# Two steps of lead between the engines of an edge network, in place of one

## The chip, the cores and the metric

The kernel runs on one core of a Trainium2 chip. The metric is the device time of one execution in microseconds, and a kernel's time is the median of its runs.

## The reference

Four graph networks run one after the other on a graph of 12,500 nodes with 128 features and 212,500 edges (sorted by destination, self-loops among them). The change touches only the second of them. It computes, for h the normalized node features:

```python
edge_input = jnp.concatenate([x[row], x[col], edge_attr], axis=-1)
h = jax.nn.silu(edge_input @ eW1 + eb1)
m_ij = jax.nn.silu(h @ eW2 + eb2)
agg = jax.ops.segment_sum(m_ij, row, num_segments=x.shape[0])
```

Here row is the source node of an edge, col its destination, and edge_attr has 16 numbers an edge. Then agg goes through a node network. Everything is float32.

## The kernel before, in words

The kernel works the whole computation in one program of many blocks. A block gives each engine its own list of instructions, and semaphores order them. Ahead of the edge network, the program has sorted the edges by source into buckets of 112 nodes and cut them into 1776 tiles of 128 edges (KT). It wrote a record for each edge to the table `rec_d` in HBM: 16 attributes, the destination's number, and the place of the source within its bucket. It also multiplied the node features with the two halves of eW1 once a node, into the tables `tab` (destination's part) and `tab_b` (source's part). So the first layer of an edge is a sum of one gathered row of `tab`, one row picked out of a 112-row window of `tab_b`, and the attributes' product.

The block of the edge network, printed below, goes over 444 quads of four tiles. Quad n uses slot s = n % 8 of a ring of eight (LR). Its steps are:

- SP, line 1840, brings the records of the quad (one DMA of 512 rows of 72 bytes) and, line 1843, four windows of `tab_b`. It waits until PE's first layer (`pe_z`) has finished quad n - 8, which had the slot. This is called a bring.
- POOL, line 1860, issues four indirect DMAs, one a tile, that gather the destination rows of `tab`. It waits for the records, since they hold the row numbers.
- DVE, line 1910, makes a one-hot of each edge's source within the bucket, from the record, next to the attributes: `comb`, 128 columns a tile.
- PE, line 1936, transposes `comb` into PSUM; ACT, line 1963, copies it to `combT`, one of two buffers.
- PE, lines 1927 and 1928, the first layer z: a transpose of the gathered rows, to which `a_win` times `combT` is added in PSUM. ACT, line 1968, applies silu into `h1`.
- PE, line 1943, the second layer; DVE, line 1891, adds the bias into `msg`; ACT, line 1972, silu in place.
- PE, line 1951, multiplies the messages with the one-hot (112 columns), which sums them by source node; DVE, line 1901, adds each of the four results into the 112 columns of F that begin at the tile's first node. That number is loaded from the table `bases` into registers by `at_base`.

No planner orders the work. The order is written out by hand in `step(n, s, h)` of DVE, PE and ACT: within one step, the parts for different quads follow each other, and a test `inside(n, d)` drops those that fall off the ends. Before the change PE's step n does: first layer of quad n, transposes of n + 1, second layer of n - 1, message sums of n - 2. DVE's step n does: bias of n - 1, adds of n - 2, one-hots of n + 2. ACT's step n does: copy of n + 1, silu of n, silu of n - 1. Each buffer between two engines (`combT`, `h1`, `msg` and the PSUM banks) is double. `steps` runs 55 turns of a hardware loop of eight steps, with 4 steps written out ahead of it and 4 behind.

Of the kernel before, what the change touches and what calls it, by code (L numbers as in the profile page):

```python
# [29 lines left out]
P = 128  # L30
# [24 lines left out]
BW = 112  # L55
NB = NP // BW
RW = 18
RQ = 4
KT = 1776
LR = 8  # L60
NT_B = (KT + P - 1) // P
NQ = KT // RQ
# [19 lines left out]
def build(nc, t, out, stop=99):  # L82
    ctx = ExitStack()
    with ctx:
# [48 lines left out]
        ident = sb("ident", [P, P])  # L133
        iota_row = sb("iota_row", [P, P])
# [23 lines left out]
        def fslot(n):  # L158
# [432 lines left out]
        W = [wts[:, n * P:(n + 1) * P] for n in range(5)]  # L591
# [3 lines left out]
        def tile_of(buf, j, w=P):  # L595
            return buf[:, j * w:(j + 1) * w]
# [1204 lines left out]
        if stop <= 6: return  # L1801

        CW = P + 2
        at[0] = 0
        comb = [in_hs(RQ * CW) for _ in range(LR)]
        a_win = [hs[:, at[0] + s * RQ * P:at[0] + (s + 1) * RQ * P] for s in range(LR)]
# [2 lines left out]
        combT = [wk[:, (LR + d) * RQ * P:(LR + d + 1) * RQ * P] for d in range(2)]  # L1809
        h1, msg = ([in_hs(RQ * P) for _ in range(2)] for _ in range(2))  # L1810
# [3 lines left out]
        with nc.Block() as block:  # L1814
# [15 lines left out]
        at_base = lambda n, eng: nc.values_load_multi_w_load_instructions(  # L1830
            bases[0:1, bass.ds(n * RQ, RQ)], engines=[eng], min_val=0, max_val=NP,
            skip_runtime_bounds_check_because="the table holds first nodes of buckets")[1]
        with nc.Block() as block:
# [35 lines left out]

            def steps(eng, step):  # L1870

                for n in range(-2, 2):
                    step(n, n % LR, n // LR)
                with eng.Fori(0, (NQ - 4) // LR) as i:
                    for u in range(LR):
                        step(i * LR + u + 2, (u + 2) % LR, i + (u + 2) // LR)
                for n in range(NQ - 2, NQ + 2):
                    step(n, n % LR, n // LR)

            inside = lambda n, d: not isinstance(n, int) or 0 <= n + d < NQ  # L1880
            round_of = lambda n, h, s, d: h + (s + d) // LR

            @block.vector
            def _(v):
                def step(n, s, h):

                    if inside(n, -1):
                        d = (s - 1) % 2
                        v.wait_ge(pe_m.sem, pe_m.after(n))
                        v.wait_ge(pe_s.sem, pe_s.after(n - 2))  # L1890
                        v.tensor_tensor(msg[d].rearrange("p (u f) -> p u f", f=P), bank(4 + d).rearrange("p (u f) -> p u f", f=P),  # L1891
                                        every(bias_b[1], RQ), ALU.add).then_inc(z2_ready.sem, 1)
                    if inside(n, -2):
                        d = s % 2
                        first = at_base(n - 2, mybir.EngineType.DVE)
                        v.wait_ge(pe_s.sem, pe_s.after(n - 1))
                        for u in range(RQ):
                            cols = F[:, bass.ds(first[u], BW)]

                            v.wait_ge(added.sem, added.after((n - 2) * RQ + u))  # L1900
                            v.tensor_tensor(cols, cols, PS[:, (6 + d) * 512 + u * BW:(6 + d) * 512 + (u + 1) * BW], ALU.add)\  # L1901
                                .then_inc(added.sem, 1)
                    if inside(n, 2):
                        s2 = (s + 2) % LR
                        v.wait_ge(rec_in[s2].sem, rec_in[s2].after((round_of(n, h, s, 2) + 1) * 16))

                        v.wait_ge(pe_s.sem, pe_s.after(n + 3 - LR))
                        for u in range(RQ):
                            c = u * CW
                            last = v.tensor_scalar(comb[s2][:, c:c + BW], iota_row[:, 0:BW], comb[s2][:, c + P + 1:c + P + 2], None,  # L1910
                                                   ALU.is_equal)
                        last.then_inc(onehot_ready.sem, 1)
                steps(v, step)

            @block.tensor
            def _(pe):
                def step(n, s, h):
                    d = s % 2
                    if inside(n, 0):

                        pe.wait_ge(turned_in.sem, turned_in.after(n + 1))
                        pe.wait_ge(win_in[s].sem, win_in[s].after((h + 1) * (16 * RQ)))
                        pe.wait_ge(got[s].sem, got[s].after((h + 1) * (16 * RQ)))
# [6 lines left out]
                    if inside(n, 1):  # L1930
                        s1 = (s + 1) % LR
                        pe.wait_ge(onehot_ready.sem, onehot_ready.after(n + 2))
                        pe.wait_ge(rec_in[s1].sem, rec_in[s1].after((round_of(n, h, s, 1) + 1) * 16))
                        pe.wait_ge(turned_in.sem, turned_in.after(n))
                        for u in range(RQ):
                            last = pe.transpose(tile_of(bank(2 + s1 % 2), u), comb[s1][:, u * CW:u * CW + P], ident[:, :])  # L1936
                        last.then_inc(pe_t.sem, 1)
                    if inside(n, -1):
                        d1 = (s - 1) % 2
                        pe.wait_ge(h1_ready.sem, h1_ready.after(n))  # L1940
                        pe.wait_ge(z2_ready.sem, z2_ready.after(n - 2))
                        for u in range(RQ):
                            last = pe.matmul(tile_of(bank(4 + d1), u), tile_of(h1[d1], u), W[2], start=True, stop=True)
                        last.then_inc(pe_m.sem, 1)
                    if inside(n, -2):
                        s2 = (s - 2) % LR
                        pe.wait_ge(msg_ready.sem, msg_ready.after(n - 1))
                        pe.wait_ge(added.sem, added.after((n - 3) * RQ))
                        for u in range(RQ):
                            c = (6 + d) * 512 + u * BW  # L1950
                            last = pe.matmul(PS[:, c:c + BW], tile_of(msg[d], u), comb[s2][:, u * CW:u * CW + BW],
                                             start=True, stop=True)
                        last.then_inc(pe_s.sem, 1)
                steps(pe, step)

            @block.scalar
            def _(act):
                def step(n, s, h):
                    if inside(n, 1):
                        d1 = (s + 1) % 2  # L1960
                        act.wait_ge(pe_t.sem, pe_t.after(n + 2))
                        act.wait_ge(pe_z.sem, pe_z.after(n))
                        act.copy(combT[d1], bank(2 + d1)).then_inc(turned_in.sem, 1)
                    if inside(n, 0):
                        d = s % 2
# [3 lines left out]
                    if inside(n, -1):  # L1969
                        d = (s - 1) % 2  # L1970
                        act.wait_ge(z2_ready.sem, z2_ready.after(n))
# [446 lines left out]
```

## Time and profile before

| | |
|---|---|
| median of 3 runs | 19,315.99 us (19,311.27 to 19,325.33) |
| profiled execution: its time | 19,314.88 us |
| profiled execution: span | 19,313.1 us |
| busy in the span: PE / PE weight loads / DVE / ACT / POOL | 7930.3 / 6299.9 / 6589.2 / 1534.9 / 11,514.0 us |
| the edge network's block | about 8446 to 11,862 us of the span |

Engines: PE is TensorE (its weight loads, PEld, overlap its matmuls), DVE VectorE, ACT ScalarE, POOL GpSimd, SP the engine that only issues DMAs here. A line such as L1936 is a line of the kernel. "idle before" is the time in which the engine did nothing ahead of these instructions, and behind "<-" stands what ended it: an instruction or a DMA, "issue" where the profile shows nothing, "remote" where a semaphore rose at that moment but the profile can't tell by whom. A queue's name ends in q (SPq). Matmuls in float32 show as more instructions than the code has. The clock is the share of full speed that TensorE was granted; 1.00 is 2.4 GHz, 0.50 is 1.2 GHz.

### The profile page before, as it was taken

To read this page: it belongs to the slowest core of one execution; us is meant where nothing else is said; L and a number is where in the kernel's file an instruction comes from. 1 tells how busy PE (TensorE), PEld (TensorE's weight loads), DVE (VectorE), ACT (ScalarE), POOL (GpSimd) and SP (SyncE) were. 2 spreads that over 40 slices of the span, in tenths; PEclk is the share of its full clock that TensorE was granted. 3 is DMA by queue.
4 is the path that set the end of the run, shared out by engine and by line. 5 is a ranking of instruction groups with operands and counts; after the bars stand their busy time and mean duration, and the time that the engine had idled before them with its cause. 6 is when DMAs were issued, how large, how long until landed. Compare 5 with 4: busy or idle time off the path is not lost. (4 is left out here: it accounts for less than half of the span.)

```text
span 19313.1 us, 144155 instructions
## 1 busy us (share of the span) xinstructions
PE 7930.3 (41%) x37282; PEld 6299.9 (33%) x37282; DVE 6589.2 (34%) x14435; ACT 1534.9 (8%) x3978; POOL 11514.0 (60%) x12117
## 2 busy tenths in 40 slices
PE   2222222222223333335565555444454444345444
PEld 1222222222222111125555554333333333233333
DVE  4444443444444333323333334222232222322222
ACT  3000000000000100012222222000000000100000
POOL 4666664666664666664454444666656666466666
PEclk5555555555555555568888887555555555555555
DMA  5222223111111111122222223111111111111112
GB/s 139 54 52 52 52 52 53 45 44 44 44 45 31 18 26 28 23 44 70 68 71 70 68 69 71 47 47 47 60 52 47 47 46 47 39 53 47 46 47 56
DMA packets 1301502, 993.98 MB, mean 51 GB/s; under 512 B 751003, under 2 KB 1121912, under 8 KB 1298942
## 3 DMA queue, kind: packets, MB, share of 16 engines
q0 software_dynamic: 387456, 692.11, 14.4%
q1 hardware_dynamic: 691046, 272.90, 6.0%
q10 hardware_dynamic: 222520, 23.31, 0.9%
q8 instruction: 211, 3.46, 0.1%
q14 instruction: 269, 2.20, 0.0%
HBM read 868.44 MB, written 132.38 MB: 52 GB/s over the span
## 5 line engine op out<-in xcount | busy, mean ns | idle before, releaser
L819 POOL DMA_INDIRECT wk<-tab,srcT x4992 | 4709.8, 943 | 2535.3 <-issue 1460.1
L920 POOL DMA_INDIRECT hs<-tab_g,srcT x3328 | 3148.0, 946 | 1886.0 <-issue 951.2
L843 PE MATMUL PS<-wk 128*128 128x128 f32 x9984 | 2579.5, 439 | 3757.3 <-DMA wk<-tab,srcT 3666.1
L843 PEld LDWEIGHTS PS<-wk 128*128 128x128 f32 x9984 | 2208.5, 325 | 4389.6 <-DMA wk<-tab,srcT 4281.8
L872 DVE TENSOR_TENSOR F<-F,PS 128x512 f32 x1248 | 857.3, 687 | 5475.2 <-PE PS L843 3723.9
L1860 POOL DMA_INDIRECT wk<-tab,hs x1776 | 1677.3, 944 | 1722.4 <-DMA hs<-rec_d 1128.2
L1780 POOL DMA_INDIRECT rec_d<-hs x1664 | 1621.1, 974 | 827.2 <-issue 522.1
L1111 DVE TENSOR_TENSOR F<-F,PS 128x126 f32 x3328 | 950.4, 286 | 2571.2 <-issue 1188.1
L1067 PE MATMUL PS<-wk,hs 128*128 128x128 f32 x6656 | 1276.4, 370 | 740.4 <-DVE hs L1096 562.3
L1067 PEld LDWEIGHTS PS<-wk,hs 128*128 128x128 f32 x6656 | 1186.4, 276 | 832.3 <-issue 777.4
L1047 PE MATMUL PS<-ident,wk 128*128 128x128 f32 (+1 forms) x104 | 45.2, 435 | 2245.9 <-ACT wk L991 2141.5
L1936 PE MATMUL PS<-ident,hs 128*128 128x128 f32 x1776 | 360.6, 337 | 1440.4 <-DVE hs L1910 1230.0
L1767 PE MATMUL PS<-hs 128*128 128x448 bf16 x416 | 225.1, 541 | 1585.5 <-DVE hs L1651 1010.0
L1891 DVE TENSOR_TENSOR hs<-PS,wts 128x512 f32<-128x512 f32 x444 | 307.0, 691 | 1477.9 <-remote 661.8
L834 PE MATMUL PS<-wk 1*128 1x512 bf16 x1248 | 745.8, 598 | 131.0 <-DVE wk L784 130.2
L784 DVE TENSOR_TENSOR wk<-PS,locT 128x1024 f32<-128x1024 f32 x624 | 758.9, 1217 | 0.1
L1047 PEld LDWEIGHTS PS<-ident,wk 128*128 128x128 f32 (+1 forms) x104 | 14.8, 142 | 2274.1 <-ACT wk L991 2169.3
L1901 DVE TENSOR_TENSOR F<-F,PS 128x112 f32 x1776 | 481.4, 271 | 798.6 <-remote 429.0
L1936 PEld LDWEIGHTS PS<-ident,hs 128*128 128x128 f32 x1776 | 232.5, 167 | 1522.6 <-DVE hs L1910 985.5
L1651 DVE TENSOR_TENSOR hs<-PS,hs 128x448 f32<-128x448 f32 x416 | 256.4, 616 | 1200.1 <-remote 1007.3
L1928 PE MATMUL PS<-wk,hs 128*128 128x128 f32 x3552 | 653.2, 286 | 0.0
L1767 PEld LDWEIGHTS PS<-hs 128*128 128x128 bf16 x416 | 43.0, 103 | 1829.7 <-DVE hs L1651 1140.1
(398 smaller groups left out, 11156.9 us busy)
## 6 DMA issues: line engine op xcount, KB each, us to landing
hs<-tab_b SPq DMA_DIRECT2D x1776, 56.0 KB
wk<-tab,srcT POOLq DMA_INDIRECT x4992
hs<-tab_g,srcT POOLq DMA_INDIRECT x3328
wk<-tab,hs POOLq DMA_INDIRECT x1776
rec_d<-hs POOLq DMA_INDIRECT x1664
rec_d<-F SPq DMA_DIRECT2D x1, 15984.0 KB
hs<-rec_d SPq DMA_DIRECT2D x444, 36.0 KB
hs<-attr_d ACTq DMA_DIRECT2D x208, 64.0 KB
```

The lines of the kernel that those rows point to most:

```text
L784: return v.tensor_tensor(dst, iota_ps[:, 0:w].unsqueeze(1).broadcast_to([P, HALF, w]), loc.unsqueeze(2).broadcast_to([P, HALF, w]), ALU.is ...
L819: pool.indirect_dma_start(gbuf[g % 4 * QUAD + u], None, table, bass.IndirectOffsetOnAxis(srcT[:, edges_of(k)], 0))\
L834: pe.matmul(bank(g % NBK), zeros[:, 0:P], zeros, start=True, stop=False, skip_group_check=True)
L843: last = pe.matmul(to, rows[u], onehot[j], start=False, stop=u == QUAD - 1, skip_group_check=True)
L872: v.tensor_tensor(cols, cols, bank(g % NBK), ALU.add).then_inc(added.sem, 1)
L920: pool.indirect_dma_start(gt[n % 2][:, j, :], None, table, bass.IndirectOffsetOnAxis(srcT[:, n * BT + j:n * BT + j + 1], 0)).then_inc(half ...
L1067: last = pe.matmul(tile_of(in_bank(g), u), gt[s][:, j, 0:D], onehot[j % (2 * HALF)], start=True, stop=True)
L1111: v.tensor_tensor(cols, cols, in_bank(k // QUAD)[:, c + 1:c + P - 1], ALU.add).then_inc(added.sem, 1)
L1780: pool.indirect_dma_start(rec_d, bass.IndirectOffsetOnAxis(slot_i[r][:, j:j + 1], 0), tile_of(rec[r], j, RW), None).then_inc(scattered[r]. ...
L1860: pool.indirect_dma_start(tile_of(b_rows[s], u), None, tab, bass.IndirectOffsetOnAxis(comb[s].bitcast(I32)[:, c:c + 1], 0))\
L1928: last = pe.matmul(z, tile_of(a_win[s], u), tile_of(combT[d], u), start=False, stop=True)
L1936: last = pe.transpose(tile_of(bank(2 + s1 % 2), u), comb[s1][:, u * CW:u * CW + P], ident[:, :])
```

## The change

The leads and lags are set by two constants, MID = 2 and FAR = 4. PE's step n does: first layer of n, transposes of n + 2, second layer of n - 2, message sums of n - 4. DVE's step n does: bias of n - 2, adds of n - 4, one-hots of n + 4. ACT's: copy of n + 2, silu of n, silu of n - 2. The buffers stay double, their index is now that of the step, and the numbers that the semaphores are compared with follow the lags. The loop takes 54 turns of eight steps, with 8 steps written out ahead and 12 behind. The programs of SP and POOL are as they were. Cut to its core:

```diff
+        MID, FAR = 2, 4
-                for n in range(-2, 2):
+                turns = (NQ - 2 * FAR) // LR
+                for n in range(-FAR, FAR):
                     step(n, n % LR, n // LR)
-                with eng.Fori(0, (NQ - 4) // LR) as i:
+                with eng.Fori(0, turns) as i:
...
-                for n in range(NQ - 2, NQ + 2):
+                for n in range(FAR + turns * LR, NQ + FAR):
...
-                    if inside(n, -1):
-                        d = (s - 1) % 2
-                        v.wait_ge(pe_m.sem, pe_m.after(n))
-                        v.wait_ge(pe_s.sem, pe_s.after(n - 2))
+                    if inside(n, -MID):
+                        d = s % 2
+                        v.wait_ge(pe_m.sem, pe_m.after(n - MID + 1))
+                        v.wait_ge(pe_s.sem, pe_s.after(n - MID - 1))
...
-                    if inside(n, -2):
+                    if inside(n, -FAR):
...
-                        v.wait_ge(pe_s.sem, pe_s.after(n - 1))
+                        v.wait_ge(pe_s.sem, pe_s.after(n - FAR + 1))
...
-                        v.wait_ge(pe_s.sem, pe_s.after(n + 3 - LR))
+                        v.wait_ge(pe_s.sem, pe_s.after(n + FAR + 1 - LR))
...
-                        pe.wait_ge(onehot_ready.sem, onehot_ready.after(n + 2))
+                        pe.wait_ge(onehot_ready.sem, onehot_ready.after(n + MID + 1))
...
-                        pe.wait_ge(turned_in.sem, turned_in.after(n))
+                        pe.wait_ge(turned_in.sem, turned_in.after(n + MID - 1))
...
-                        pe.wait_ge(h1_ready.sem, h1_ready.after(n))
-                        pe.wait_ge(z2_ready.sem, z2_ready.after(n - 2))
+                        pe.wait_ge(h1_ready.sem, h1_ready.after(n - MID + 1))
+                        pe.wait_ge(z2_ready.sem, z2_ready.after(n - MID - 1))
...
-                        pe.wait_ge(msg_ready.sem, msg_ready.after(n - 1))
-                        pe.wait_ge(added.sem, added.after((n - 3) * RQ))
+                        pe.wait_ge(msg_ready.sem, msg_ready.after(n - FAR + 1))
+                        pe.wait_ge(added.sem, added.after((n - FAR - 1) * RQ))
```

## Rows read from the trace of the kernel before

**Rows 1.** Groups by line in the edge network's stretch (8440 to 11870): busy us, mean ns | idle before.
```profile
L1860 POOL DMA_INDIRECT wk<-tab,hs x1776 | 1677.3, 944 | 1722.4 <-DMA hs<-rec_d 1128.2 <-issue 523.5 <-PE PS L1928 70.7
...
L1927 PE MATMUL PS<-ident,wk 128*128 128x128 f32 x1776 | 512.1, 288 | 36.3 <-issue 21.0 <-ACT wk L1963 15.2
...
L1936 PE MATMUL PS<-ident,hs 128*128 128x128 f32 x1776 | 360.6, 337 | 1440.4 <-DVE hs L1910 1230.0 <-issue 210.4
```

**Rows 2.** Waits of SP's queue there: total us, times, longest us.
```profile
SPq L1840 <- remote: 775.3, 155, 9.5
SPq L1840 <- PE PS L1928: 718.6, 199, 6.1
```

**Rows 3.** Timeline of SP: start us, length us, issues; the 1st, 16th and 444th bring.
```profile
8444.47 0.00 SPq L1840 DMA_DIRECT2D hs<-rec_d  x1
...
8540.19 0.39 SPq L1840 DMA_DIRECT2D hs<-rec_d  x1
...
11808.12 0.40 SPq L1840 DMA_DIRECT2D hs<-rec_d  x1
```

**Rows 4.** Stretches: length, busy us (instructions) of PE, PEld, DVE, ACT, POOL, clock, DMA, GB/s.
```profile
8544.00:11808.00 3264.00, 1925.74 (x13665) 1842.67 (x13664) 1088.39 (x3840) 728.38 (x1280) 1612.17 (x1707) 0.83 0.30 69
11824.00:11855.00 31.00, 23.57 (x204) 22.46 (x202) 16.01 (x57) 10.52 (x19) 0.00 (x0) 1.00 0.00 1
...
8800.00:9200.00 400.00, 233.92 (x1690) 223.32 (x1689) 134.53 (x477) 90.07 (x159) 198.97 (x212) 0.84 0.29 70
10000.00:10400.00 400.00, 239.36 (x1686) 228.84 (x1685) 134.93 (x474) 89.99 (x159) 200.31 (x212) 0.83 0.29 70
```

**Rows 5.** Timeline of PE and DVE, one of the last quads: start, length, [idle before].
```profile
11831.00 0.66 PE L1936 MATMUL PS<-ident,hs 128*128 128x128 f32 x4 [1.29 <-DVE hs L1910]
...
11833.66 1.48 DVE L1901 TENSOR_TENSOR F<-F,PS 128x112 f32 x4 [0.37 <-PE PS L1951]
...
11835.08 0.84 DVE L1910 TENSOR_SCALAR hs<-iota_row,hs 128x112 f32<-128x112 f32 x4
...
11836.17 0.63 PE L1936 MATMUL PS<-ident,hs 128*128 128x128 f32 x4 [1.41 <-DVE hs L1910]
```

**Rows 6.** Timeline of all engines from 9008 to 9025, a long quad.
```profile
9008.53 1.87 SPq L1843 DMA_DIRECT2D hs<-tab_b  x4
...
9010.81 0.94 POOL L1860 DMA_INDIRECT wk<-tab,hs  x1 [4.82 <-DMA hs<-rec_d]
...
9013.60 4.60 SPq L1843 DMA_DIRECT2D hs<-tab_b  x4
...
9013.81 0.66 PE L1936 MATMUL PS<-ident,hs 128*128 128x128 f32 x4 [1.18 <-DVE hs L1910]
...
9014.30 1.06 PE L1943 MATMUL PS<-wts,hs 128*128 128x128 f32 x8
...
9019.72 0.94 POOL L1860 DMA_INDIRECT wk<-tab,hs  x1 [0.30 <-issue]
9020.82 0.69 DVE L1891 TENSOR_TENSOR hs<-PS,wts 128x512 f32<-128x512 f32 x1 [7.07 <-remote]
...
9024.90 1.11 PE L1936 MATMUL PS<-ident,hs 128*128 128x128 f32 x4 [7.33 <-DVE hs L1910]
```

**Rows 7.** Timeline in the earlier stage that scatters the records.
```profile
7023.05 0.97 POOL L1780 DMA_INDIRECT rec_d<-hs  x1 [0.30 <-issue]
7023.07 0.62 DVE L1651 TENSOR_TENSOR hs<-PS,hs 128x448 f32<-128x448 f32 x1 [19.91 <-remote]
```

**Rows 8.** Timelines of PE and POOL in the opening of the edge network.
```profile
8455.32 0.63 PE L1928 MATMUL PS<-wk,hs 128*128 128x128 f32 x2
...
8466.56 0.95 POOL L1860 DMA_INDIRECT wk<-tab,hs  x1 [5.17 <-PE PS L1928]
...
8505.63 0.98 POOL L1860 DMA_INDIRECT wk<-tab,hs  x1 [5.27 <-PE PS L1928]
...
8543.65 0.39 PE L1928 MATMUL PS<-wk,hs 128*128 128x128 f32 x2
```

More of the change, by code:

```diff
@@ L1870, in steps @@
             def steps(eng, step):
-                for n in range(-2, 2):
+                turns = (NQ - 2 * FAR) // LR
+                for n in range(-FAR, FAR):
                     step(n, n % LR, n // LR)
-                with eng.Fori(0, (NQ - 4) // LR) as i:
+                with eng.Fori(0, turns) as i:
                     for u in range(LR):
-                        step(i * LR + u + 2, (u + 2) % LR, i + (u + 2) // LR)
-                for n in range(NQ - 2, NQ + 2):
+                        step(i * LR + u + FAR, (u + FAR) % LR, i + (u + FAR) // LR)
+                for n in range(FAR + turns * LR, NQ + FAR):
                     step(n, n % LR, n // LR)
@@ L1892, in step @@
                                         every(bias_b[1], RQ), ALU.add).then_inc(z2_ready.sem, 1)
-                    if inside(n, -2):
+                    if inside(n, -FAR):
                         d = s % 2
-                        first = at_base(n - 2, mybir.EngineType.DVE)
-                        v.wait_ge(pe_s.sem, pe_s.after(n - 1))
+                        first = at_base(n - FAR, mybir.EngineType.DVE)
+                        v.wait_ge(pe_s.sem, pe_s.after(n - FAR + 1))
                         for u in range(RQ):
@@ L1898, in step @@
                             cols = F[:, bass.ds(first[u], BW)]
-                            v.wait_ge(added.sem, added.after((n - 2) * RQ + u))
+                            v.wait_ge(added.sem, added.after((n - FAR) * RQ + u))
                             v.tensor_tensor(cols, cols, PS[:, (6 + d) * 512 + u * BW:(6 + d) * 512 + (u + 1) * BW], ALU.add)\
                                 .then_inc(added.sem, 1)
-                    if inside(n, 2):
-                        s2 = (s + 2) % LR
-                        v.wait_ge(rec_in[s2].sem, rec_in[s2].after((round_of(n, h, s, 2) + 1) * 16))
-                        v.wait_ge(pe_s.sem, pe_s.after(n + 3 - LR))
+                    if inside(n, FAR):
+                        s4 = (s + FAR) % LR
+                        v.wait_ge(rec_in[s4].sem, rec_in[s4].after((round_of(n, h, s, FAR) + 1) * 16))
+                        v.wait_ge(pe_s.sem, pe_s.after(n + FAR + 1 - LR))
@@ L1908, in step @@
                         for u in range(RQ):
                             c = u * CW
-                            last = v.tensor_scalar(comb[s2][:, c:c + BW], iota_row[:, 0:BW], comb[s2][:, c + P + 1:c + P + 2], None,
+                            last = v.tensor_scalar(comb[s4][:, c:c + BW], iota_row[:, 0:BW], comb[s4][:, c + P + 1:c + P + 2], None,
                                                    ALU.is_equal)
@@ L1929, in step @@
                         last.then_inc(pe_z.sem, 1)
-                    if inside(n, 1):
-                        s1 = (s + 1) % LR
-                        pe.wait_ge(onehot_ready.sem, onehot_ready.after(n + 2))
-                        pe.wait_ge(rec_in[s1].sem, rec_in[s1].after((round_of(n, h, s, 1) + 1) * 16))
-                        pe.wait_ge(turned_in.sem, turned_in.after(n))
+                    if inside(n, MID):
+                        s2 = (s + MID) % LR
+                        pe.wait_ge(onehot_ready.sem, onehot_ready.after(n + MID + 1))
+                        pe.wait_ge(rec_in[s2].sem, rec_in[s2].after((round_of(n, h, s, MID) + 1) * 16))
+                        pe.wait_ge(turned_in.sem, turned_in.after(n + MID - 1))
@@ L1935, in step @@
                         for u in range(RQ):
-                            last = pe.transpose(tile_of(bank(2 + s1 % 2), u), comb[s1][:, u * CW:u * CW + P], ident[:, :])
+                            last = pe.transpose(tile_of(bank(2 + d), u), comb[s2][:, u * CW:u * CW + P], ident[:, :])
                         last.then_inc(pe_t.sem, 1)
-                    if inside(n, -1):
-                        d1 = (s - 1) % 2
-                        pe.wait_ge(h1_ready.sem, h1_ready.after(n))
-                        pe.wait_ge(z2_ready.sem, z2_ready.after(n - 2))
+                    if inside(n, -MID):
+                        pe.wait_ge(h1_ready.sem, h1_ready.after(n - MID + 1))
+                        pe.wait_ge(z2_ready.sem, z2_ready.after(n - MID - 1))
@@ L1942, in step @@
                         for u in range(RQ):
-                            last = pe.matmul(tile_of(bank(4 + d1), u), tile_of(h1[d1], u), W[2], start=True, stop=True)
+                            last = pe.matmul(tile_of(bank(4 + d), u), tile_of(h1[d], u), W[2], start=True, stop=True)
                         last.then_inc(pe_m.sem, 1)
-                    if inside(n, -2):
-                        s2 = (s - 2) % LR
-                        pe.wait_ge(msg_ready.sem, msg_ready.after(n - 1))
-                        pe.wait_ge(added.sem, added.after((n - 3) * RQ))
+                    if inside(n, -FAR):
+                        s4 = (s - FAR) % LR
+                        pe.wait_ge(msg_ready.sem, msg_ready.after(n - FAR + 1))
+                        pe.wait_ge(added.sem, added.after((n - FAR - 1) * RQ))
@@ L1949, in step @@
                         for u in range(RQ):
                             c = (6 + d) * 512 + u * BW
-                            last = pe.matmul(PS[:, c:c + BW], tile_of(msg[d], u), comb[s2][:, u * CW:u * CW + BW],
+                            last = pe.matmul(PS[:, c:c + BW], tile_of(msg[d], u), comb[s4][:, u * CW:u * CW + BW],
                                              start=True, stop=True)
@@ L1958, in step @@
                 def step(n, s, h):
[L1959 to L1963, printed above, removed]
+                    d = s % 2
+                    if inside(n, MID):
+                        act.wait_ge(pe_t.sem, pe_t.after(n + MID + 1))
+                        act.wait_ge(pe_z.sem, pe_z.after(n + MID - 1))
+                        act.copy(combT[d], bank(2 + d)).then_inc(turned_in.sem, 1)
                     if inside(n, 0):
-                        d = s % 2
                         act.wait_ge(pe_z.sem, pe_z.after(n + 1))
@@ L1968, in step @@
                         act.activation(h1[d], bank(d), ACT.Silu).then_inc(h1_ready.sem, 1)
-                    if inside(n, -1):
-                        d = (s - 1) % 2
-                        act.wait_ge(z2_ready.sem, z2_ready.after(n))
+                    if inside(n, -MID):
+                        act.wait_ge(z2_ready.sem, z2_ready.after(n - MID + 1))
                         act.activation(msg[d], msg[d], ACT.Silu).then_inc(msg_ready.sem, 1)
```

## The prediction

> **What bounds the kernel now.** I looked first at the groups by line in the stretch of the edge network, since the diff touches nothing else. It lasts from about 8446 to 11862 us, 3416 us of the span, for 444 quads. PE waits for nothing but one thing there: the transposes of line 1936, ahead of which it idles 1440.4 us, 1230.0 us of that until DVE's one-hots of line 1910. Ahead of the first layer's products (line 1927), where the gathered rows are waited for, it idles 36.3 us [rows 1]. So gathers are in time, and POOL is not late: it idles 1722.4 us, mostly until the records of the slot that it is to fill have landed. Those are brought by SP, and SP waits 718.6 us for PE's first layer to free the slot and 775.3 us for the same semaphore with the releaser shown as "remote" [rows 2]. The ring of eight slots is thus full, and PE's chain sets the pace.
>
> The table of stretches gives that pace. Between the 16th bring (8540.19) and the last (11808.12) lie 428 quads in 3267.9 us, 7.635 us a quad [rows 3]. In 3264 us PE is busy 1925.74 us, that is 4.5 us a quad at a mean clock of 0.83; DVE 1088.39 (2.5), ACT 728.38 (1.7), POOL 1612.17 [rows 4]. No engine is full.
>
> The timeline then shows two kinds of quad. At the very end, where nothing is brought or gathered, one quad follows another in 5.17 us (11831.00 to 11836.17), and the chain is plain: the sums' matmuls end, DVE adds four tiles (11833.66, 1.48 us), makes four one-hots (11835.08, 0.84 us), PE transposes at 11836.17 after 1.41 us idle [rows 5]. PE itself works 23.57 us in 31 us there, 204 matmuls at 32 a quad, so 3.7 us a quad at full clock [rows 4].
>
> In the middle every second or third quad is far longer, as the one whose transposes come at 9013.81 and the next at 9024.90, 11.1 us later. PE starts the second layer at 9014.30 and takes 1.06 us, and DVE, which waits for just that, starts at 9020.82, after 7.07 us of idle "<-remote": PE's signal came 5.5 us late. PE's next transposes, which need DVE's one-hots, wait 7.33 us and run at the low clock (1.11 us, against 0.66 before). In the same microseconds SP's four issues of line 1843 take 4.60 us in place of 1.87, and POOL gathers without a break, eight in a row (9010.81 to 9019.72); its stop and the late signal come together [rows 6]. A clean bring of SP (9008.53) fell into a break of POOL. I read this as **a freeze**: where SP brings while POOL gathers back to back, signals of PE arrive late and SP crawls. It isn't a matter of PE's load: in the earlier stage that scatters the records, where PE has little to do, DVE waits 19.91 us "<-remote" (to 7023.07) in a run of POOL that still goes on at 7023.05, with 0.30 us between scatters [rows 7].
>
> **The change part by part.**
> 1. Slack. Today PE's step n needs the one-hots, first layer and messages of step n-1 of DVE and ACT; after the change those of step n-2. The 1.41 us ahead of the transposes in a clean quad goes, and the step falls to what is busiest: PE 3.7 us [rows 4], DVE 0.69 + 1.48 + 0.84 = 3.0 us plus its gaps [rows 5, 6], POOL 4 x (0.944 + 0.30) = 4.98 us [rows 1, 6]. By this POOL's 4.98 us is the floor.
> 2. In a freeze PE can go on two steps in place of one before it starves, and DVE has up to two steps of released work.
> 3. What is late next: SP's brings. Nothing of SP or POOL is moved, no DMA and no queue; but the opening shows what the two do when PE doesn't hold them. There SP has free slots, and 15 brings take from 8444.47 to 8540.19, 6.38 us a quad [rows 3]; POOL gathers 12 times, stops some 5 us (5.17 at 8466.56, 5.27 at 8505.63), and so on [rows 8]. That is the pace of bring and gather against one another, and I take it for the pace after: 6.38 us. It is bounded below by POOL's 4.98 and above, short of a loss (rival C), by today's 7.635. I take 6.38 because it is measured in this very loop with both at work, and because PE can just follow: two runs and stops of POOL lie between 8466.56 and 8505.63, 19.5 us for each 12 gathers [rows 8], in which three quads need 3 x 3.7 us of PE and about 3 x 3.5 of DVE (an estimate, the 3.0 with gaps), and of the 19.5 us a freeze leaves the 5 us stop, the 3 us until the next sets in, and two steps carried over.
> 4. Costs. The one-hots of quad n+4 reuse a slot whose last reader is the message sum of quad n-4, which DVE's adds just ahead wait for anyway: no new wait. The semaphore waits, register loads and instructions of a step stay as many; 20 steps stand outside the loop in place of 8, which I cost at nothing, since each step is the same instructions (0 to 3 us). At the end four quads' sums are left in place of two; the last of DVE's bias and four adds cost 0.69 + 1.48 us a quad [rows 5, 6], some 3 us more after what PE's saved gaps hide; 0 to 10. At the start four one-hots are made ahead, under the same first records, POOL's first gathers and SP's first brings: nothing.
>
> The sum, for the profiled execution's 19314.88 us (span 19313.1, and within 1.2 us of the median): 428 x (7.635 - 6.38) = 537 us off, 3 us on: **18,781 us**. The opening and the last eight quads I leave as they are.
>
> A rule that can be set against this: the Trainium skill, page "DMA: Bandwidth & Descriptors", section "SWDGE vs HWDGE vs iDMA", has it that transfers issued by SP don't touch the descriptor rings that GpSimd writes, and are immune to what disturbs those. By that rule alone nothing should slow SP's brings, and the floor would be POOL's. The trace disagrees on the outcome, with 4.60 against 1.87 us for the same four issues; no row shows which part of the chip they meet in.
>
> **The rivals.**
> A. *The pace is held from outside, and stays.* For it: the pace is steady over long stretches: 400 us from 8800 and 400 us from 10000 hold 1690 and 1686 matmuls [rows 4]; it is as if freezes came after so many transfers and gave out a fixed rate. Then a smoother pipeline only brings the next freeze sooner. Against: in the opening brings went through at 6.38 us, and 7.6 us also comes out of POOL's 5.0 a quad and one stop of 5 us for every two quads. Time: 19,318, with a spread of 60 us either way, since 0.1 us a quad is already 43 us.
> B. *No collision counts once PE has slack; POOL is the bound.* 428 x (7.635 - 4.98) = 1136 us off, 3 on: 18,182. For it: the stops of POOL are then rare, and the ring of eight can cover a freeze. Against: the opening had free slots too, and POOL stopped every 12 gathers.
> C. *Slower: longer runs of POOL make longer freezes.* The place is the run-and-stop cycle. In the opening, the first layer's products of quad 0 begin their last pair at 8455.32 and those of quad 8 at 8543.65 [rows 8], 11.0 us a quad, 1.8 quads to a cycle of 19.5 us: PE was slower under POOL's continuous run than it is now. Slack gives POOL these runs back. The point that decides is 19.5 / 7.635 = 2.55 quads a cycle: if PE gets fewer than that with slack two, the time goes up. At 2.4 it is 8.13 us a quad, 428 x 0.49 = 210 us on: 19,528 with the 3 of the end. Against: a full ring stops POOL, and that brings back the present pattern.
>
> **How the numbers follow.** My forecast's case (5.4 to 7.3 us a quad, 18,360 to 19,170) gets 0.55, A 0.25, B 0.07, C 0.13. The range: 18,300 to 19,350 takes in the first, nearly all of A, and leaves out B, much of C and the first case's tail, some 0.2. A measurement of this kernel can tell 0.2% (39 us) from nothing. Faster by more: 0.55 + 0.07 + 0.07 of A = 0.69. Within: 0.15 of A and 0.01 of C, 0.16. Slower: 0.03 of A and 0.12 of C, 0.15.
>
> **What would show it.** Right: the stretch shrinks from 3416 to about 2880 us; the idle time before line 1936 falls from 1440 to under 500 us, and part of it turns up before line 1927 as a wait for the gathers; POOL's runs grow to 12 gathers and its idle falls under 1300 us; brings come every 6.4 us; SP's waits for line 1928 shrink. A shows as the same 7.6 us with the idle time moved to another line of PE. B shows as POOL without stops. C shows as runs of 12 and more with under 2.5 quads to each. The forecast is wrong if "remote" waits fill the two steps of slack each time, or if the loop's pace in the opening was set by something that only the opening has.

## The result and the profile after

| | before | after |
|---|---|---|
| median | 19,320.66 us (4 runs) | 19,000.15 us (4 runs, 18,990.61 to 19,016.99) |
| profiled execution: its time | 19,314.88 us | 18,990.61 us |
| profiled execution: span | 19,313.1 us | 18,988.8 us |
| ratio after / before | | 0.9838, interval 0.9827 to 0.9850 |

The change wins 320 us. The direction was forecast, and the time lies in the range, which was 1050 us wide; the gain is 320 of the 534 us forecast.

The lines of the code have moved by one to five: POOL's gathers are L1861, SP's brings L1841 and L1844, DVE's bias, adds and one-hots L1893, L1903 and L1912, PE's first layer L1929 and L1930, transposes L1938, second layer L1944, sums L1952, ACT's copy L1964. First the groups by line in the edge network (8440 to 11600), to be held against [rows 1]:

```profile
L1861 POOL DMA_INDIRECT wk<-tab,hs x1776 | 1685.6, 949 | 1410.6 <-DMA hs<-rec_d 731.0 <-issue 533.6 <-PE PS L1930 133.3
L1930 PE MATMUL PS<-wk,hs 128*128 128x128 f32 x3552 | 807.7, 317 | 296.0 <-issue 294.1
...
L1944 PE MATMUL PS<-wts,hs 128*128 128x128 f32 x3552 | 645.0, 327 | 157.2 <-issue 155.5
L1952 PE MATMUL PS<-hs 128*128 128x112 f32 x3552 | 598.3, 312 | 121.5 <-issue 118.9 <-DVE F L1903 1.7
...
L1929 PE MATMUL PS<-ident,wk 128*128 128x128 f32 x1776 | 551.0, 310 | 141.0 <-issue 134.6 <-ACT hs L1968 4.4 <-DMA wk<-tab,hs 1.0
...
L1938 PE MATMUL PS<-ident,hs 128*128 128x128 f32 x1776 | 360.5, 325 | 204.7 <-issue 124.2 <-DVE hs L1912 80.1
L1893 DVE TENSOR_TENSOR hs<-PS,wts 128x512 f32<-128x512 f32 x444 | 306.5, 690 | 1762.0 <-remote 1530.5 <-PE PS L1952 128.3 <-issue 97.1
```

The idle time ahead of the transposes is down from 1440.4 to 204.7 us. PE waits for hardly anything any more (80.1 us for the one-hots, of which 72 are the wait for the first quad's). DVE's late signals have not gone: its bias waits 1530.5 us for "remote", against 661.8 before. They only no longer hold PE. And yet it idles 920 us in all (296.0 + 157.2 + 121.5 + 141.0 + 204.7), nearly all of it "issue": the profile shows nothing that it waited for, in the midst of its lists of matmuls.

SP's waits there answer to [rows 2]. Ahead of a bring SP waits for one semaphore only, that of PE's first layer, so both lines are waits for a slot of the ring: 26.2 us are put down to PE, 921.2 to "remote". What has changed is that the slot is mostly free by then and the signal late. Of the 416 brings from the 25th to the 440th, 317 start over 2 us after the end of the first layer that frees their slot (half of them over 4.9 us after it); before it was 150, and half started within 0.8 us.

```profile
SPq L1841 <- remote: 921.2, 216, 12.1
...
SPq L1841 <- PE PS L1930: 26.2, 20, 2.0
```

Then SP's timeline at the 16th and the 444th bring [rows 3], and the same loop as a stretch [rows 4]:

```profile
8535.92 0.39 SPq L1841 DMA_DIRECT2D hs<-rec_d  x1
...
11496.34 0.40 SPq L1841 DMA_DIRECT2D hs<-rec_d  x1
```

```profile
8547.00:11481.00 2934.00, 2139.16 (x13495) 1971.00 (x13495) 1065.74 (x3799) 719.53 (x1268) 1607.30 (x1694) 0.80 0.34 76
```

2960.4 us for 428 quads are **6.92 us a quad**, against 7.635. The bookkeeping closes: the brings gain 3267.9 - 2960.4 = 307.5 us. From the last bring to the last add there are 40.5 us (to 11536.8) in place of 54.2 (to 11862.3), 14 more. And the first bring comes at 8439.93 in place of 8444.47, 4.5 us that the change has no part in. That is 326, and the two profiled executions differ by 324. Where did the rest of the removed wait go? 1236 us went from the idle time ahead of the transposes (1440.4 to 204.7). Of these, 679 came back as idle time ahead of PE's other lines (296.0 + 157.2 + 121.5 + 141.0 = 715.7, against the 36.3 of line 1927 before, [rows 1]), and 213 as slower instructions (PE is busy 2139.16 us in the stretch, 1925.74 before [rows 4]; the transposes of the gathered rows take 310 ns in place of 288). That leaves 344, near the 321 that the brings and the end gain.

Last, the timeline of all engines around one freeze, which answers to [rows 6]:

```profile
9500.98 1.06 PE L1944 MATMUL PS<-wts,hs 128*128 128x128 f32 x8
...
9503.77 0.23 PEld L1929 LDWEIGHTS PS<-ident,wk 128*128 128x128 f32 x1
9504.22 0.95 POOL L1861 DMA_INDIRECT wk<-tab,hs  x1 [0.30 <-issue]
9505.17 0.27 PE L1929 MATMUL PS<-ident,wk 128*128 128x128 f32 x1 [1.04 <-issue]
9505.18 0.19 PEld L1930 LDWEIGHTS PS<-wk,hs 128*128 128x128 f32 x1 [1.19 <-issue]
...
9505.90 0.19 PEld L1930 LDWEIGHTS PS<-wk,hs 128*128 128x128 f32 x1 [0.53 <-issue]
...
9506.61 0.37 PE L1930 MATMUL PS<-wk,hs 128*128 128x128 f32 x1 [1.05 <-issue]
...
9507.32 0.18 PEld L1938 LDWEIGHTS PS<-ident,hs 128*128 128x128 f32 x1 [1.24 <-issue]
9508.02 1.01 PE L1938 MATMUL PS<-ident,hs 128*128 128x128 f32 x4 [1.04 <-issue]
...
9508.16 0.59 ACT L1964 COPY wk<-PS 128x512 f32<-128x512 f32 x1 [7.79 <-remote]
9508.27 0.69 DVE L1893 TENSOR_TENSOR hs<-PS,wts 128x512 f32<-128x512 f32 x1 [6.30 <-remote]
...
9508.83 1.91 PE L1944 MATMUL PS<-wts,hs 128*128 128x128 f32 x8
...
9509.45 0.95 POOL L1861 DMA_INDIRECT wk<-tab,hs  x1 [3.04 <-DMA hs<-rec_d]
```

Here is what the added slack ran into. While POOL gathers, ACT and DVE get no signal (7.79 and 6.30 us "<-remote"), as before: the second layer that DVE's bias waits for ended at 9502.04 (9500.98 + 1.06), and the bias starts at 9508.27. PE now has work left that waits for neither, and begins it. But its own instructions, matmuls and weight loads alike, then start only in steps of 0.70 us or twice that: 9503.77, 9505.17, 9505.90, 9506.61, 9507.32, 9508.02. POOL's run ends at 9506.41 (9509.45 less its 3.04 idle), and 1.6 us later all three go on together. The matmuls behind it run at the half clock: eight in 1.91 us, where eight take 1.06 at full clock [rows 6], and the granted clock of that stretch is 0.50:

```profile
9508.00:9510.00 2.00, 1.98 (x10) 1.97 (x10) 1.45 (x4) 1.84 (x4) 0.55 (x1) 0.50 0.23 67
```

This is no single case. Counted over the whole loop, 899 of PE's idle gaps, 643 us, stand ahead of matmuls that wait for no semaphore. In the kernel before there is not one. In its long quads PE stood at its wait for the one-hots when the slow stretch would have come (idle from 9017.57 to 9024.90 [rows 6]), so this could not be seen in its trace.

The rows of before hold one more fact that bears on the forecast's idea of a freeze. In the earlier stage of [rows 7], PE's transposes of line 1737 end at 6999.20 (6998.78 + 0.42), and ACT's copy of them starts at 7019.57, 20 us later, in a run of POOL's scatters:

```profile
6998.78 0.42 PE L1737 MATMUL PS<-ident,F 128*128 128x128 f32 x1
...
7019.57 0.91 ACT L1616 COPY wk<-PS 128x896 f32<-128x896 f32 x1 [24.23 <-remote]
```

From 7000 to 7025 us SP issues nothing at all. The issues of that stretch are these:

```profile
rec_d<-hs POOLq DMA_INDIRECT x19
hs<-attr_d ACTq DMA_DIRECT2D x2, 64.0 KB
```

So a signal of PE comes late there without any bring of SP.

### The profile page after: what moved, and what is told of

The parts are those of the page before. It is cut to its first block and busy times, and to the rows that moved or that the text cites. A ratio compares the mean times of both kernels' runs of the same rounds, so it can differ in the third digit from the quotient of the medians.

```text
span 18988.8 us, 142973 instructions
## 1 busy us (share of the span) xinstructions
PE 8166.6 (43%) x37282; PEld 6450.6 (34%) x37282; DVE 6582.3 (35%) x14435; ACT 1534.0 (8%) x3978; POOL 11546.0 (61%) x12117
## 5 line engine op out<-in xcount | busy, mean ns | idle before, releaser
L819 POOL DMA_INDIRECT wk<-tab,srcT x4992 | 4720.8, 946 | 2526.4 <-issue 1460.2
L1861 POOL DMA_INDIRECT wk<-tab,hs x1776 | 1685.6, 949 | 1410.6 <-DMA hs<-rec_d 731.0
L1067 PE MATMUL PS<-wk,hs 128*128 128x128 f32 x6656 | 1275.5, 370 | 737.4 <-DVE hs L1096 578.1
L1067 PEld LDWEIGHTS PS<-wk,hs 128*128 128x128 f32 x6656 | 1185.6, 276 | 829.5 <-issue 769.0
L1930 PE MATMUL PS<-wk,hs 128*128 128x128 f32 x3552 | 807.7, 317 | 296.0 <-issue 294.1
L1893 DVE TENSOR_TENSOR hs<-PS,wts 128x512 f32<-128x512 f32 x444 | 306.5, 690 | 1762.0 <-remote 1530.5
L1930 PEld LDWEIGHTS PS<-wk,hs 128*128 128x128 f32 x3552 | 664.4, 227 | 347.7 <-issue 346.4
L1944 PE MATMUL PS<-wts,hs 128*128 128x128 f32 x3552 | 645.0, 327 | 157.2 <-issue 155.5
L1952 PE MATMUL PS<-hs 128*128 128x112 f32 x3552 | 598.3, 312 | 121.5 <-issue 118.9
```

The costliest lines, as they stand in the source:

```text
L819: pool.indirect_dma_start(gbuf[g % 4 * QUAD + u], None, table, bass.IndirectOffsetOnAxis(srcT[:, edges_of(k)], 0))\
L1067: last = pe.matmul(tile_of(in_bank(g), u), gt[s][:, j, 0:D], onehot[j % (2 * HALF)], start=True, stop=True)
L1861: pool.indirect_dma_start(tile_of(b_rows[s], u), None, tab, bass.IndirectOffsetOnAxis(comb[s].bitcast(I32)[:, c:c + 1], 0))\
L1944: last = pe.matmul(tile_of(bank(4 + d), u), tile_of(h1[d], u), W[2], start=True, stop=True)
```

## The experiments

They were run in four groups, each on one chip with the kernel before beside it, and every ratio is against the kernel before of its own group. That took 19,332.8 us in the first group (runs e1 to e4), 19,323.3 in the second (e5 to e8), 19,328.5 in the last (e12), and **16,057.4 us** in the third (e9 to e11), which fell on another chip. The second group and e12 had the same chip, the first a different one with the same kernel time. "Pace" is us a quad over the 414 quads between the ends of the first layer of the 17th and of the 431st; it is 7.63 for before and 6.93 for after, counted so.

**e1: only the two leads ahead of the first layer.** The constants are split in four; one-hots four ahead and transposes two ahead, as after; second layer one and sums two behind, as before.

```diff
-        MID, FAR = 2, 4
+        OH, TR, L2, SC = 4, 2, 1, 2
```

> One-hots four quads ahead and turning two ahead as in the changed kernel, but the second layer one quad and the message sums two quads behind, as before. If slack counts as the smallest lag on any of PE's waits, the lag of one step that stays on the second layer and the sums keeps PE tied to the last step of ACT and DVE: under a quarter of the 320 us gained, 19,240 us or more. Rival: the trace of before shows PE waiting only for the one-hots, so this half alone brings the gain: about 19,000 us.

Measured: 19,032.53 us, ratio 0.9840 (0.9823 to 0.9856), pace 6.96. The second layer and the sums of PE, groups by line of this run:

```profile
L1945 PE MATMUL PS<-wts,hs 128*128 128x128 f32 x3552 | 646.5, 327 | 186.9 <-issue 162.4 <-ACT hs L1971 21.9 <-DVE hs L1893 0.8
L1954 PE MATMUL PS<-hs 128*128 128x112 f32 x3552 | 604.6, 315 | 156.9 <-issue 125.3 <-ACT hs L1975 21.5 <-DVE F L1903 8.7
```

Half of the change gives all of its gain that can be told from noise (0.9840 against 0.9838 and, in e12, 0.9847). The smallest lag of the four doesn't count: with a lag of one PE waits for `h1` and `msg` 43 us in all.

**e2: only the two lags behind.**

```diff
-        MID, FAR = 2, 4
+        OH, TR, L2, SC = 2, 1, 2, 4
```

> The other half alone: second layer two and message sums four quads behind, one-hots two and turning one ahead as before. By the theory of the smallest lag: PE still waits for the one-hots of the step before, no gain, 19,280 to 19,330 us. Rival, that late signals on the way back (second layer to bias to sums) are what costs: about 19,100 us.

Measured: 19,335.67 us, ratio 0.9997 (0.9988 to 1.0007), pace 7.59. The wait of before is all there, ahead of the transposes:

```profile
L1938 PE MATMUL PS<-ident,hs 128*128 128x128 f32 x1776 | 351.9, 331 | 1426.3 <-DVE hs L1912 1142.3 <-issue 284.1
```

DVE's one-hots stand last in its step, behind the bias that waits for PE's late signal. Only where they are made further ahead does PE not wait for them; what DVE and ACT owe PE behind the first layer came in time at both lags tried (e1). So the other half of the change does nothing by itself.

**e7: the one-hots alone, one quad further ahead.**

```diff
-        MID, FAR = 2, 4
+        OH, TR, L2, SC = 3, 1, 1, 2
```

> The kernel before with one thing changed: one-hots three quads ahead in place of two; turning one ahead, second layer one and sums two behind as before. The one-hots that PE waits for come then from DVE's step before the last. If that wait alone was the cost: 19,000 to 19,070 us. If the copy of the turned one-hots, which still comes from the step before and needs a signal of PE, takes its place: 19,200 to 19,320 us, with the idle time moved to the first layer's line.

Measured: 19,140.73 us, ratio 0.9903 (0.9887 to 0.9920), pace 7.24: some 183 of 300 us. The wait has moved to the next thing that is only one step ahead, ACT's copy of the transposed one-hots:

```profile
L1929 PE MATMUL PS<-ident,wk 128*128 128x128 f32 x1776 | 623.6, 351 | 988.3 <-ACT wk L1967 960.4 <-issue 28.0
```

So one more quad of lead for the one-hots brings part of the gain, and the rest comes with the lead of the transposes and the fourth quad of the one-hots (e1, pace 6.96). These two were not taken apart.

**e3: after, without POOL's gathers.** POOL's block and PE's wait for it are left out, so the first layer adds whatever is in the rows' buffers.

```diff
-            @block.gpsimd
-            def _(pool):
-                def gather(n, s, i):
...
-                        pe.wait_ge(got[s].sem, got[s].after((h + 1) * (16 * RQ)))
```

> The changed kernel with the gathers of POOL left out in the edge network (the first layer reads what stands in the buffers; the output is not the reference's). If POOL's back-to-back gathers cause the freezes, waits shown as remote nearly vanish, SP's issues take 1.87 us each four, and the pace is PE's 3.7 to 4.3 us a quad: stage 1650 to 1950 us, total 17,550 to 17,850 us. If the pace is held by something else (a rate of records or transfers, of which gathers are a small part), quads still take over 6 us: 18,600 us or more.

Measured: 17,498.41 us, ratio 0.9048 (0.9030 to 0.9066), pace 3.54. A stretch of it, same columns as [rows 4]:

```profile
8600.00:9000.00 400.00, 400.00 (x3619) 400.00 (x3618) 286.22 (x1017) 205.00 (x339) 0.00 (x0) 1.00 0.35 77
```

In this stretch PE is never idle, at full clock; in the whole block no wait of PE's matmuls, of DVE or of ACT is shown as "remote" or "issue". SP's four issues take 1.87 us all but three times (all in the first eleven quads). The freezes of this block come with POOL's gathers. Whether it is POOL's issuing or the transfers that it starts, the run can't tell, as both are gone.

**e6: before, without POOL's gathers** (the same part left out).

> The kernel before, with POOL's gathers left out (output not the reference's). Without freezes its chain shows alone: the 5.0 to 5.2 us a quad of the last quads of its trace, so the stage takes 2230 to 2320 us and the kernel 18,130 to 18,230 us, against 17,498 for the changed kernel without gathers. If instead the chain costs nothing without freezes, both are equal: 17,500 us.

Measured: 18,143.66 us, ratio 0.9387 (0.9368 to 0.9405), pace 5.00. PE's transposes:

```profile
L1916 PE MATMUL PS<-ident,hs 128*128 128x128 f32 x1776 | 290.8, 286 | 619.8 <-DVE hs L1891 548.7 <-DMA hs<-rec_d 71.1
```

Where nothing freezes and no gather bounds, the slack is worth 18,144 - 17,498 = 645 us (two chips, whose kernel before differs by 10 us), 1.45 us a quad, and it is the gap ahead of the transposes of [rows 5] that goes.

**e5: after, without SP's windows.** SP's four transfers of `tab_b` a quad and PE's wait for them are left out, so the first layer adds whatever stands in the windows' buffers; records are still brought.

```diff
-                    for u in range(RQ):
-                        sp.dma_start(tile_of(a_win[s], u)[0:BW, :], tab_b[bass.ds(first[u], BW), :]).then_inc(win_in[s].sem, 16)
...
-                        pe.wait_ge(win_in[s].sem, win_in[s].after((h + 1) * (16 * RQ)))
```

> The changed kernel without SP's four window transfers a quad (the first layer reads what stands in the buffers; the output is not the reference's); records and gathers stay. If a bring beside back-to-back gathers makes the freeze, four fifths of SP's issues gone leave few freezes: under 5.8 us a quad, 18,500 us or less. If POOL's gathers alone make it, freezes stay nearly as they were: 6.3 to 6.9 us a quad, 18,700 to 19,000 us.

Measured: 18,972.51 us, ratio 0.9815 (0.9796 to 0.9835), pace 6.86. The changed kernel on the same chip (e12) takes 19,031.85 us at a pace of 7.01.

```profile
L1891 DVE TENSOR_TENSOR hs<-PS,wts 128x512 f32<-128x512 f32 x444 | 306.2, 690 | 1753.5 <-remote 1503.1 <-PE PS L1949 177.2 <-PE PS L1941 40.2
```

The late signals cost as much without four fifths of SP's transfers (1503.1 us; 1530.5 in after, 1553.6 in e12), and the kernel is only 59 us faster. The window transfers are not what makes them. The one record transfer a quad is still there; against it as the cause speaks the earlier stage, where SP issues nothing and a signal is 20 us late.

**e4: after, with a stop of POOL before every quad.** It waits until its own last four gathers have landed.

```diff
                 def gather(n, s, i):
+                    if not (isinstance(n, int) and n == 0):
+                        b = (s - 1) % LR
+                        pool.wait_ge(got[b].sem, got[b].after((i + (1 if s else 0)) * (16 * RQ)))
```

> The changed kernel in which POOL waits, ahead of a quad's gathers, until the gathers of the quad before have landed: a stop of some 2 us after every four. If long runs of back-to-back gathers make the freezes: remote waits of DVE fall from 1530 us to under 400, and the pace is 5.0 plus the stop, 6.7 to 7.3 us a quad: 18,900 to 19,150 us. If any gather beside a bring is enough: remote waits stay over 1000 us and the stops add to them, over 7.5 us a quad, 19,250 us or more.

Measured: 19,188.30 us, ratio 0.9922 (0.9906 to 0.9939), pace 7.28.

```profile
L1934 PE MATMUL PS<-ident,wk 128*128 128x128 f32 x1776 | 605.5, 341 | 1144.3 <-DMA wk<-tab,hs 1142.6 <-ACT hs L1973 1.7
...
L1898 DVE TENSOR_TENSOR hs<-PS,wts 128x512 f32<-128x512 f32 x444 | 306.9, 691 | 1938.9 <-PE PS L1957 1063.6 <-remote 794.3 <-issue 58.9
```

This lies between the two ranges of the expectation. Runs of four halve the "remote" time (794.3, not under 400) and take PE's slow stretches away altogether: not one of its gaps stands ahead of a matmul that waits for nothing. But the stops are dearer than that: now PE waits 1142.6 us for the gathers.

**e8: the same stop before every second quad only.**

```diff
+                    if s % 2 == 0 and not (isinstance(n, int) and n == 0):
```

> The changed kernel in which POOL waits for the landing of all its gathers ahead of every second quad: a stop of some 2.5 us after each eight. If the short stop ends a freeze as the long stops do: 10 us of gathers and 2.5 for two quads, 6.3 to 6.7 us a quad, 18,720 to 18,900 us. If a freeze builds up within eight gathers whatever stands between the runs: as the changed kernel or a little slower, 18,980 to 19,150 us.

Measured: 18,899.28 us, ratio 0.9779 (0.9762 to 0.9795), pace 6.71. Two of POOL's stops in its timeline, with 8 gathers between:

```profile
9520.96 0.94 POOL L1864 DMA_INDIRECT wk<-tab,hs  x1 [3.15 <-DMA wk<-tab,hs]
...
9533.14 0.94 POOL L1864 DMA_INDIRECT wk<-tab,hs  x1 [2.42 <-remote]
```

This is the fastest version where the freezes are, 133 us under the changed kernel on the same chip (e12). POOL stops anyway; where the stop is made to come after eight gathers it is shorter. Counted over the loop, e8 has 241 stops of more than 1 us with 3.4 us in the mean, e12 has 219 with 4.3: 815 us against 936, and the difference of 121 is near the 133. PE's slow stretches are still there (744 gaps, 541 us). That the shorter stops are the reason was not tested by itself.

**e9, e10, e11: the third group, on the other chip.** e9 is before with e8's stop; e10 is after with a stop at three slots of eight; e11 is after with two of a quad's four gathers (the other two tiles keep whatever is in their buffers).

```diff
+                    if s in (0, 3, 6) and not (isinstance(n, int) and n == 0):
```

```diff
-                    for u in range(RQ):
+                    for u in range(RQ // 2):
```

> The kernel before with the stop of the pairs (POOL waits for its landings ahead of every second quad). In the kernel before POOL stops anyway, two times in three quads, for want of records. If the stop only helps where PE has slack: 19,280 to 19,400 us, no gain. If shorter freezes help by themselves, the gain of 100 us seen on the changed kernel appears here too: 19,180 to 19,260 us.

> The changed kernel with the stop ahead of three quads in eight (slots 0, 3, 6), so after runs of 8 to 12 gathers. If the cost of a freeze grows with the length of the run, it lies between the pairs and the changed kernel: 18,900 to 19,000 us. If only the number of stops counts, fewer forced stops are better than the pairs: under 18,880 us.

> The changed kernel with two gathers a quad in place of four (the first layer of the other two tiles reads what stands in the buffers; output not the reference's). If freezes need long back-to-back runs, POOL, now 2.5 us a quad, is never pressed and they vanish: 3.5 to 4.0 us a quad, 17,500 to 17,750 us. If each gather costs its share, 0.85 us (6.92 less 3.54 over four): 5.2 us a quad, 18,150 to 18,350 us.

Measured, against 16,057.36 us: e9 16,580.50, ratio 1.0325 (1.0308 to 1.0343), pace 6.24; e10 16,446.18, ratio 1.0242 (1.0225 to 1.0259), pace 5.90; e11 15,372.34, ratio 0.9573 (0.9554 to 0.9592), pace 3.54. All three expectations were made for a chip with freezes, and here there were none: no wait of any engine is shown as "remote" in any of the three traces. So none of the three answers its question. The groups of e9 and of e10 that tell it:

```profile
L819 POOL DMA_INDIRECT wk<-tab,srcT x4992 | 4710.3, 944 | 1697.3 <-issue 1520.1
...
L1896 DVE TENSOR_TENSOR hs<-PS,wts 128x512 f32<-128x512 f32 x444 | 307.2, 692 | 1299.2 <-PE PS L1948 1293.4 <-issue 5.8
```

```profile
L1934 PE MATMUL PS<-ident,wk 128*128 128x128 f32 x1776 | 566.9, 319 | 721.5 <-DMA wk<-tab,hs 720.2 <-issue 0.2
```

DVE waits for PE by name. Each instruction takes what it takes elsewhere (944 ns a gather, 690 an addition of the bias); only the waits are gone, in stages that the change doesn't touch as well. There a forced stop of POOL is pure loss, and the gain of e8 turns into 3.25% lost with the leads of before. What e11 was to tell, whether half as many gathers freeze half as much, can't be told here.

The kernel before left no trace on that chip, but its pace can be estimated in two ways. From e9: 523 us over 428 quads are 1.22, so 6.24 - 1.22 = 5.02. From e11: 685 us over 444 quads are 1.54, so 3.54 + 1.54 = 5.08. That is about POOL's 4.98 [rows 1, 6], and also the 5.00 of e6. For the changed kernel e10 gives an estimate: eight quads take 8 x 5.90 = 47.2 us, its three stops (2.7 us in the mean of all 175, of which 0.3 stands between any two gathers) are 7.2 of them, and the other 40.0 are 5.0 a quad, with PE waiting for hardly anything but the gathers (720.2 us). By these estimates both kernels run at POOL's pace there, and the change would bring next to nothing.

**e12: the changed kernel, unaltered, once more.**

> The changed kernel unaltered, once more. The run tells whether the gain of the change belongs to the freezes. Theory: with the freezes (the kernel before takes some 19,320 us on that chip), the change again gives 0.984, 18,980 to 19,030 us, 6.9 us a quad in the edge network. Where the freezes are absent (the kernel before takes some 16,057 us, as in the last three runs), nobody makes PE late: before, POOL's gathers (4 x about 1.25 us = 5.0 us a quad) would already be the bound, as PE's own step without gathers took 5.0 us with the leads of before and 3.5 with those of after; then the change can win little or nothing: ratio 0.99 to 1.003, POOL without stops, and no wait shown as 'remote'. Rival (the slack is worth its 1.4 us a quad everywhere, as without gathers): ratio 0.96 where the freezes are absent, 15,450 us.

Measured: 19,031.85 us, ratio 0.9847 (0.9831 to 0.9864), pace 7.01, beside 19,328.46 of before. It fell on a chip with freezes, and repeats the result. What the change does without them wasn't measured.

## Why the forecast was right in its direction and too large

- **What bounds the kernel**: right. PE's wait for the one-hots was the path: e2, which leaves the leads ahead of the first layer as they were, wins nothing, and e1, which changes only them, wins it all.
- **Step 1, slack**: right in kind, and without freezes nearly exact: e3 gives PE 3.54 us a quad (forecast 3.7), and the gap ahead of the transposes goes (1.45 us a quad between e6 and e3, forecast 1.41). What it takes as one, that PE needs the whole step before of DVE and ACT, e1 and e2 take apart: only the leads ahead of the first layer count.
- **Step 2, PE goes on two steps in a freeze**: this failed. PE was taken for an engine that a freeze only stops through its semaphores. It is slowed itself, to an instruction each 0.70 us: 899 gaps, 643 us of idle time, where before there was none.
- **Step 3, the pace after**: the term that was mis-sized. It was put at 6.38 us, from the opening; it measures 6.917. 428 x 0.537 = 230 us on, the end's 17 off and the 4.5 by which the block starts earlier make 18,990 of the 18,781: the profiled execution's time. The opening itself repeated (15 brings in 95.99 us, before in 95.72), but there each slot has been free for 11 us or more (27 or more after the change), so SP waits for no signal. In the steady loop most brings wait for the signal of a first layer. PE is slowed in most runs of POOL, and the signal is late besides (SP's 921.2 us). Runs of 12 gathers and a stop were forecast; counted through the loop they are 221 runs of 8.0 on average (before 298 of 6.0).
- **"SP brings while POOL gathers back to back"** as the cause: half wrong. e3 shows POOL's gathers to be needed, e5 shows SP's windows not to be, and the earlier stage of [rows 7] has a late signal with no issue of SP. The rule set against it, of the Trainium skill, page "DMA: Bandwidth & Descriptors", section "SWDGE vs HWDGE vs iDMA" (SP's transfers don't touch the rings that GpSimd writes), is thus not what the runs speak against. It says what can't disturb SP's transfers by way of those rings; here it is the issuing of SP and PE alike that slows, and by what way no run shows.
- **Step 4, the costs**: forecast 3 us on at the end; measured 14 us off. That the last quads too run with the slack fits this, but was not tested. The 20 steps outside the loop cost nothing that can be seen.
- **Rival A** (the pace is held from outside) fell with the pace. **Rival B** (POOL the bound) fell here; the estimate of 5.0 to 5.1 us a quad for the chip without freezes is where it would hold. **Rival C** (longer runs of POOL, slower) fell: runs grew from 6.0 to 8.0, and PE got 2.0 quads to each cycle of run and stop (444 / 221), but a cycle was some 14 us long (the 3097 us of the block / 221), not the 19.5 assumed.
- **What would show it**: the idle time ahead of the transposes fell under 500 us as forecast, but turned up as "issue", not as a wait for the gathers; POOL's idle time fell to 1410.6, not under 1300; the brings come each 6.9, not 6.4 us; the stretch shrank to 3097, not to 2880 us. One sign that was named for being wrong came true in part: "remote" waits of DVE's bias grew from 661.8 to 1530.5 us, though PE waits for them no longer.
- **The number**: that the time lies in the range owes something to the range's width. The gain is six tenths of the forecast, and the pace it was added up from did not come.

What stays open: by what POOL's gathers hold up the signals and the issuing of other engines, and why one chip of those met here doesn't show it; and what the change is worth there. If both kernels run at POOL's bound there, as the estimates have it, the change can bring little; no run shows it.

## What to carry to other kernels

Look at where each step stands in its engine's list: lead was worth adding here where an instruction that others wait for stands behind one whose signal comes late (the one-hots), and nothing elsewhere (e1, e2), so split such a change and time its halves. Before crediting slack with hiding a stall, ask whether the engine that is to go on is free of the same stall; a trace in which it stands at a semaphore can't show that. And a spacing that is tuned to a stall of some chips (e8, 0.9779) can cost where the stall is absent (e9, 1.0325).

## What the runs showed of the hardware

- On two of three chips, back-to-back indirect DMAs of GpSimd (one each 1.25 us, runs of eight) delay semaphore signals between other engines by some 6 us (9502.04 to 9508.27 above), and slow the issuing of PE to one instruction in 0.70 us and that of SP's four DMAs from 1.87 us to 4.60 [rows 6]. Without them all of this is gone in that block (e3); with runs of four (e4) PE's slow issuing is gone and the late signals are half. Leaving the gathers out saves the changed kernel 18,990 - 17,497 = 1493 us (two profiled executions of different groups), POOL's own bound included.
- This depends on the chip, or on its condition: the third group is the only one of its chip. The kernel before takes 19,323 to 19,333 us in three groups, on two chips, and 16,057 in the third group. POOL's idle time ahead of L819, in a stage far from the change, is 1697.3 us there (e9), and here, in the page of after:

```profile
L819 POOL DMA_INDIRECT wk<-tab,srcT x4992 | 4720.8, 946 | 2526.4 <-issue 1460.2
```

- PE's matmuls right behind the freeze above run at half clock: the eight at 9508.83 take 1.91 us, at a granted clock of 0.50. The mean clock of the loop fell from 0.83 [rows 4] to 0.80 though PE is busier, and in e3, where PE never pauses, it is 1.00.
